# Layer 0 for four pairs at once in a conditional two-layer kernel, with the loads of x, the rings and two waits moved to fit

## The reference

```python
# layer 0: x is (128, 64, 512), w[subject] is 64x64, bias[subject] is 64
x = x + einsum('bct,bcd->bdt', x, weights[subjects]) + bias[subjects][:, :, None]
# layer 1: W is 512x512, A[k] is 16x512, Bm[k] is 512x16, scalings[k] a number
H = einsum('btd,od->bto', x, W)
delta = einsum('btr,bor->bto', einsum('btd,brd->btr', x, A[k]), Bm[k]) * scalings[k]
x = x + H + delta
```

## Time and profile before

| | value |
|---|---|
| median of three runs | 265.81 us |
| profiled execution | 265.84 us |
| its span | 264.2 us |
| TensorE busy | 241.5 us, 91% |
| VectorE, ScalarE, GpSimd busy | 145.2, 113.4, 82.2 us |
| mean granted TensorE clock | 0.978 |
| DMA | 36.69 MB, 139 GB/s in the mean |
| chain of waits, by engine | PE 86%, DVE 5%, DMA 3% |

### The profile page before, as it was taken

How to read it: one execution, slowest core, us unless ns; L and a number is a source line. 1 busy time by engine, 2 the same in 40 slices (tenths; PEclk the granted TensorE clock), 3 DMA queues, 4 the chain that set the end, 5 groups by cost and what they waited for, 6 DMA issues and landing times.

```text
span 264.2 us, 9940 instructions
## 1 busy us (share of the span) xinstructions
PE 241.5 (91%) x2929; PEld 194.7 (74%) x2930; DVE 145.2 (55%) x244; ACT 113.4 (43%) x189; POOL 82.2 (31%) x284
## 2 busy tenths in 40 slices
PE   0463999899999999999999999999999999999993
PEld 0442888688788888888888887888878887887882
DVE  5657557755565666755575655566675554433200
ACT  2154345544454445444464444544544443333411
POOL 6332342533324333332343332432333333320000
PEclk9977699999999999999999999999999999999999
DMA  6663144555545554655455545555564445552231
GB/s 114 152 186 105 43 133 134 160 139 148 154 144 156 157 159 139 180 154 144 121 177 155 141 140 146 157 152 159 139 188 149 144 127 179 155 156 79 70 78 42
DMA packets 25826, 36.69 MB, mean 139 GB/s; under 512 B 6736, under 2 KB 8784, under 8 KB 25808
## 3 DMA queue, kind: packets, MB, share of 16 engines
q1 hardware_dynamic: 20400, 28.06, 37.2%
q10 hardware_dynamic: 5408, 8.40, 12.3%
HBM read 19.67 MB, written 16.78 MB: 138 GB/s over the span
## 4 chain that ended last, share of the span: by engine, by line
PE 86%; DVE 5%; DMA 3%; issue 2%; ACT 1%; SPq 1%; ACTq 0%; DVEq 0%
PE ps L717 69%; PE ps L702 13%; PE ps L682 2%; DMA x_ring<-in_x_dram 2%; PE ps L664 2%; DVE m_lo L487 1%; DMA ids_i<-in_itok_B_dram 1%; DVE m_f L481 1%; ACT m_hi L563 1%; DVE x L494 0%; ACT x_hi L569 0%; DVE place L453 0%; DVE prec_n L388 0%; PE ps L654 0%; DVE x_lo L502 0%
## 5 line engine op out<-in xcount | busy, mean ns | idle before, releaser
L717 PE MATMUL ps<-m_hi,x_hi 128*128 x264 | 106.9, 405 | 0.8 <-DVE m_lo L487 0.8
L717 PE MATMUL ps<-m_lo,x_hi 128*128 x264 | 103.5, 392 | 0.0
L717 PE MATMUL ps<-m_hi,x_lo 128*128 x264 | 103.4, 392 | 0.0
L502 DVE TENSOR_TENSOR x_lo<-x,x_hi 128x512 fp32r<-128x512 f32 x64 | 44.5, 695 | 86.5 <-ACT x_hi L569 86.5
L359 POOL COPY p_pair<-p_all 64x64 f32 x128 | 45.6, 356 | 135.0 <-DVE x L494 62.0
L578 ACT ACTIVATE o_ring<-ps 128x512 f32<-128x512 f32 x60 | 35.8, 597 | 63.2 <-PE ps L717 62.9
L717 PEld LDWEIGHTS ps<-m_hi,x_hi 128*128 128x128 f32 x264 | 49.9, 189 | 12.6 <-issue 1.6
L717 PEld LDWEIGHTS ps<-m_hi,x_lo 128*128 128x128 f32 x264 | 49.8, 189 | 10.8
L569 ACT ACTIVATE x_hi<-x 128x512 fp32r<-128x512 f32 x64 | 40.4, 632 | 39.8 <-ACT o_ring L578 18.6
L717 PEld LDWEIGHTS ps<-m_lo,x_hi 128*128 128x128 f32 x264 | 49.9, 189 | 9.5
L702 PEld LDWEIGHTS ps<-p_pair,x_ring 64*64 64x64 f32 x2048 | 34.2, 139 | 18.2 <-issue 16.5
(11 more groups left out here) (81 smaller groups left out, 55.5 us busy)
## 6 DMA issues: line engine op xcount, KB each, us to landing
x_ring<-in_x_dram SPq DMA_DIRECT2D x128, 128.0 KB, 2.6
out_dram<-o_ring ACTq DMA_DIRECT2D x64, 128.0 KB, 2.4
out_dram<-o_ring SPq DMA_DIRECT2D x64, 128.0 KB, 2.5
o_ring<-in_L_cond_W_dram SPq DMA_DIRECT2D x4, 256.0 KB, 4.6
a_f<-in_L_cond_A_dram SPq DMA_DIRECT2D x8, 128.0 KB
b_nat<-in_L_cond_Bm_dram SPq DMA_DIRECT2D x1, 256.0 KB, 4.1
p_all<-in_L_cond_weights_dram SPq DMA_DIRECT2D x2, 128.0 KB, 4.3
bias_all<-in_fside_8xS_dram SPq DMA_DIRECT2D x1, 256.0 KB, 5.7
```

The costliest lines, as they stand in the source:

```text
L502: nc.vector.tensor_tensor(x1_lo[:, u % HELD], x1[:, u % 2], x1_hi[:, u % HELD], ALU.subtract).then_inc(x1_lo_ready, 1)
L717: mm = nc.tensor.matmul(ps[:, bank, :], part[:, u % HELD, c, :], m[:, ds(k * (TC * T) + c * T, T)], start=(c == 0 and part is x1_hi and m ...
```

## The change

It takes layer 0 for four pairs in one burst, at u = 2 and u = 6 only, for pairs j+2 to j+5 in the order j+2, j+4, j+3, j+5. The four results lie in the same four PSUM banks as before, two to a bank pair, in columns 0 to 255 and 256 to 511 (`l0_out`). `x1_add` waits for both results of its bank pair (`l0_count`).

SP loads x for the four pairs j+6 to j+9 in one step, at u = 2 and u = 6 (`load_quad`); `x_ring` still has four slots. `p_pair` and `bias_pair` have eight slots, and POOL waits for a slot accordingly. The batch numbers stand in a table of their own, `batch`, written by one DVE copy instead of two copies and a memset.

In the head, PE does both first layer-0 pairs after all four tiles of M and then `turn_b(1)`; layer 0 of pairs 2 and 3 moves from before layer 1 of pair 0 to before layer 1 of pair 1, and pairs 4 to 7 follow at pair 2. DVE and ACT make tiles 1 to 3 of M before the first `x1_add` and `x1_round`. PE's wait for M moves from u = 5 to u = 6, behind the burst. `load_a`, `a_round`, `a_split`, `turn_b` and the tiles of M keep their step.

```diff
@@ -45,9 +45,10 @@
     MIXED = K // 2
     XR = 4
     OR = 4
-    AHEAD = 6
+    PR = 8
+    L0_QUAD = 4
     HELD = 4
-    W_BATCH, W_AHEAD, W_SUBJECT, W_PLACE = 0, 2, 4, 6
+    W_SUBJECT, W_PLACE = 0, 2
 
     HEAD = 4
     BODY = 8
@@ -77,8 +78,8 @@
         w_nat = o_ring
         p_all = sb("p_all", [P, S, C])
         bias_all = sb("bias_all", [P, S, C])
-        p_pair = sb("p_pair", [P, XR, C])
-        bias_pair = sb("bias_pair", [P, XR, P])
+        p_pair = sb("p_pair", [P, PR, C])
+        bias_pair = sb("bias_pair", [P, PR, P])
         x1 = sb("x1", [P, 2, TC, P])
         x1_hi = sb("x1_hi", [P, HELD, TC, P], F32R)
         x1_lo = sb("x1_lo", [P, HELD, TC, P], F32R)
...
@@ -122,9 +124,16 @@
         ps = ctx.enter_context(nc.psum_tensor("ps", [P, 8, 512], F32))
         b_turned_at = ps[:, 4, :].rearrange("p (c n) -> p n c", c=TC)
 
-        def l0_banks(u):
-
-            return 6 * (u % 2)
+        def l0_count(j, u):
+
+            if isinstance(j, int) and j < L0_QUAD:
+                return j + 1
+            return j - u % L0_QUAD + (2, 4)[u % 2]
+
+        def l0_out(u):
+
+            cols = TC * C * (u // 2 % 2)
+            return ps[:, 6 * (u % 2):6 * (u % 2) + 2, cols:cols + TC * C]
 
 
         ids_in = sem("ids_in")
...
@@ -248,10 +251,17 @@
 
             def load_x(j, slot, b):
 
-                at_least(sp, l0_done, j - XR + 1)
+                at_least(sp, l0_done, j - XR + 1 if isinstance(j, int) and j < XR + L0_QUAD
+                         else j - XR - slot + (1, 3, 2, 4)[slot])
                 for half in range(2):
                     sp.dma_start(x_ring[C * half:C * half + C, slot, :], x[ds(b[half], 1)]
                                  .rearrange("b c t -> (b c) t")).then_inc(x_in[slot], 16)
+
+            def load_quad(j):
+
+                b = words(sp, regs, batch[0:1, ds(j * 2, 2 * L0_QUAD)], B - 1)
+                for i in (range(L0_QUAD) if isinstance(j, int) and j <= L0_QUAD else (0, 2, 1, 3)):
+                    load_x(j + i, i, b[2 * i:2 * i + 2])
 
 
             sp.wait_ge(order_ready, 1)
@@ -261,23 +271,20 @@
                          .to_broadcast([P, S * C]).rearrange("p (s d) -> p s d", s=S)).then_inc(bias_in, 16)
             load_w(3)
             sp.wait_ge(batches_ready, 1)
-            for j in range(XR):
-                load_x(j, j, words(sp, regs[:2], table[0:1, j * 8:j * 8 + 2], B - 1))
+            load_quad(0)
             load_a(1)
-            for j in range(XR, AHEAD):
-                load_x(j, j % XR, words(sp, regs[:2], table[0:1, j * 8:j * 8 + 2], B - 1))
+            load_quad(XR)
 
             def step(j, u, n):
                 if n is not None and u == HEAD - 1:
 
                     load_a(n + 2)
-                more = not isinstance(j, int) or j + AHEAD < PAIRS
-                b = words(sp, regs[:4 if more else 1], table[0:1, ds(j * 8, 4 if more else 1)], B - 1)
-                if more:
-                    load_x(j + AHEAD, (u + AHEAD) % XR, b[W_AHEAD:W_AHEAD + 2])
+                if u % L0_QUAD == 2 and (not isinstance(j, int) or j + XR + 2 < PAIRS):
+                    load_quad(j + XR + 2)
+                b, = words(sp, regs[:1], batch[0:1, ds(j * 2, 1)], B - 1)
 
                 sp.wait_ge(out_ready, j + 1)
-                sp.dma_start(out[ds(b[0], 1)].rearrange("b c t -> (b c) t"),
+                sp.dma_start(out[ds(b, 1)].rearrange("b c t -> (b c) t"),
                              o_ring[0:C, u % OR, :]).then_inc(even_out[u % OR], 16)
 
             pairs(sp, step, HEAD - 1)
@@ -350,10 +357,10 @@
                 if place_at is not None:
                     dup_b(place_at)
                     pool.wait_ge(b_dupped, place_at + 1)
-                slot = u % XR
-
-                at_least(pool, x1_ready, j - XR + 1)
-                s = words(pool, regs, table[0:1, ds(j * 8 + W_SUBJECT, 2)], S - 1)
+                slot = u % PR
+
+                at_least(pool, x1_ready, j - (PR - 1 if n is None else min(PR - 1, HEAD - 1 + (u - HEAD) % BODY)))
+                s = words(pool, regs, table[0:1, ds(j * 4 + W_SUBJECT, 2)], S - 1)
                 def place_p(half):
                     rows = slice(C * half, C * half + C)
                     nc.gpsimd.tensor_copy(p_pair[rows, slot, :], p_all[rows, ds(s[half], 1), :]
...
@@ -488,12 +491,11 @@
 
             def x1_add(j, u):
 
-                dve.wait_ge(l0_done, j + 1)
+                dve.wait_ge(l0_done, l0_count(j, u))
                 at_least(dve, x1_lo_ready, j - 1)
-                bank = l0_banks(u)
                 nc.vector.tensor_tensor(x1[:, u % 2].rearrange("p c (h d) -> p c h d", h=2),
-                                        ps[:, bank:bank + 2, 0:TC * C].rearrange("p h (c d) -> p c h d", c=TC),
-                                        bias_pair[:, u % XR, :].rearrange("p (h d) -> p h d", h=2).unsqueeze(1)
+                                        l0_out(u).rearrange("p h (c d) -> p c h d", c=TC),
+                                        bias_pair[:, u % PR, :].rearrange("p (h d) -> p h d", h=2).unsqueeze(1)
                                         .to_broadcast([P, TC, 2, C]), ALU.add).then_inc(x1_ready, 1)
 
             def x1_split(j, u):
@@ -509,25 +511,28 @@
             m_add(0, 0)
             m_add(1, 1)
             m_split(0, 0)
+            m_split(1, 1)
+            m_add(2, 2)
+            m_add(3, 3)
             x1_add(0, 0)
-            m_add(2, 2)
+            m_split(2, 2)
             x1_split(0, 0)
-            m_split(1, 1)
-            m_add(3, 3)
-            m_split(2, 2)
+            x1_add(1, 1)
             m_split(3, 3)
-            x1_add(1, 1)
             x1_split(1, 1)
 
             def step(j, u, n):
+                if n is None and j == 0:
+                    a_split(1)
+                    b_split(1)
                 if not isinstance(j, int) or j + 2 < PAIRS:
                     x1_add(j + 2, u + 2)
                     x1_split(j + 2, u + 2)
                 for place_at, chunk in split_at(j, u, n):
                     m_split(place_at * TC + chunk, chunk)
-                if makes_parts(j, u, n) is not None:
-                    a_split(makes_parts(j, u, n))
-                    b_split(makes_parts(j, u, n))
+                if n is not None and u == HEAD:
+                    a_split(n + 2)
+                    b_split(n + 2)
                 for place_at, chunk in tiles_of(j, u, n):
                     m_add(place_at * TC + chunk, chunk)
                 if n is None and j == HEAD - 1:
...
@@ -688,21 +696,29 @@
                 pe.wait_ge(x_in[slot], after(j, u, 32))
                 pe.wait_ge(pair_ready, j * 4 + 4)
 
-                at_least(pe, x1_ready, j - 1)
+                at_least(pe, x1_ready, j - 1 if isinstance(j, int) and j < L0_QUAD else j - u % L0_QUAD)
 
             def layer0(j, u):
 
                 slot = u % XR
-                bank = l0_banks(u)
+                x1_t = l0_out(u)
                 for c in range(TC):
                     for side in range(2):
                         for half in range(2):
                             rows = slice(C * half, C * half + C)
                             at = c * P + side * C
-                            mm = nc.tensor.matmul(ps[side * C:side * C + C, bank + half, c * C:c * C + C],
-                                                  x_ring[rows, slot, at:at + C], p_pair[rows, slot, :],
+                            mm = nc.tensor.matmul(x1_t[side * C:side * C + C, half, c * C:c * C + C],
+                                                  x_ring[rows, slot, at:at + C], p_pair[rows, u % PR, :],
                                                   start=True, stop=True)
                 mm.then_inc(l0_done, 1)
+
+            def l0_at(j, u):
+
+                if isinstance(j, int) and j == 1:
+                    return (1, 2)
+                if u % L0_QUAD == 2 and (not isinstance(j, int) or j + 2 < PAIRS):
+                    return (2, 4, 3, 5)
+                return ()
 
             def layer1(j, u, k, bank, done=l1_done, tiles_awaited=False):
 
@@ -727,28 +743,28 @@
             m_product(0, 0)
             m_product(1, 1)
             turn_w(2)
-            layer0_inputs(0, 0)
-            layer0(0, 0)
             turn_w(3)
             m_product(2, 2)
             m_product(3, 3)
             pe.wait_ge(others_ready, 2)
+            layer0_inputs(0, 0)
+            layer0(0, 0)
             layer0_inputs(1, 1)
             layer0(1, 1)
+            turn_b(1)
             regs = [pe.alloc_register(f"pe_word{i}") for i in range(2)]
 
             def step(j, u, n):
                 mixed = n_of_mixed(j) is not None
-                if u % 2 == 0 and (not isinstance(j, int) or j + 2 < PAIRS):
-                    layer0_inputs(j + 2, u + 2)
-                    layer0_inputs(j + 3, u + 3)
-                k = words(pe, regs[:2 if mixed else 1], table[0:1, ds(j * 8 + W_PLACE, 2 if mixed else 1)], K - 1)
```

(38 more changed lines are left out.)

## The result

The changed kernel takes **293.41 us** (median of 4 runs, 291.35 to 295.1) against 266.19 for the kernel before: a ratio of 1.102, 95% interval 1.092 to 1.113. It is slower, as forecast (290, range 272 to 299). Its profiled execution took 292.57 us.

The account below looks back on a forecast made before the run. TensorE, 91% busy, was taken to bound the kernel, with no slack on A's load path. Head -5.0, first body +2.7, five bodies +27.0, end -0.7 sum to +24 on 265.84, giving 290 us, range 272 to 299.

Parts of the forecast that it names:

- SP's queue: SP at u = 2: eight x loads take 5.4 us before the store, delaying A's load from B2 + 6.55 to 10.2.
- From A to B6: Load of A to burst at u = 6: 4.2 + 2.07 + 1.33 us plus 0.95 for extra waits; stall 4.4 us a body.
- The clock: PE's granted clock halves after the stall in each body, costing 1.4 us a body, bounds 0 and 2.5.
- The rival that the clock holds: Stalls in the loop, broken by the tile, do not lower PE's clock: 282 us instead of 290; chance 0.25.
- The other two rivals: SP's queue does not decide, 258 us, chance 0.13; or edges are bought dearly, 263 to 270 us, chance 0.10.
- The body: A loop body of eight pairs takes 33.9 us instead of 28.51, 5.4 more; five bodies 27.0.
- The first body: From the first burst of four to the next at u = 2: 32.6 us instead of 29.83, 2.7 more.
- The head: Before the loop, the first burst of four starts at 30.4 instead of 35.46: 5.0 us gained, between 3 and 6.5.
- The end: Behind the loop, three bursts' edges fewer: 0.7 us gained.
- The bursts' edges: Entering and leaving layer 0 bursts on PE costs 0.21 us together; fewer bursts gain 1.9 us, 0.7 behind the loop.
- The third rival's sum: A's load costs 1.5 us a body, clock stays: -7.7 + 9 to 12, given as 263 to 270 us; chance 0.10.

Follow-up runs that it names:

- e1: Changed kernel, but SP loads A at u = 2, ahead of the eight loads of x, instead of in the step behind them: 269.1 us, ratio 1.013.
- e2: Kernel before, but A's load issued behind the two loads of x of its step instead of ahead of them: 276.3 us, ratio 1.040.
- e8: Kernel before, but A's load issued behind the store of the step at u = 3: 283.8 us, ratio 1.076.
- e5: Changed kernel, A's load unmoved, but PE waits once for POOL's last pair and once for x1_ready before a burst of four: 292.0 us, ratio 1.101.
- e4: e1, but PE waits once for POOL's last pair and once for x1_ready before a burst of four: 260.7 us, ratio 0.983.
- e3: Changed kernel with 18 extra matmuls a body filling PE's stall at u = 5, around the first tile of M: 287.7 us, ratio 1.086.
- e6: e4, with M's first tile behind the burst of u = 6 and pair 7's x1_add ahead of the splits: 259.0 us, ratio 0.979.
- e7: Kernel before, but SP loads A in the step at u = 2, ahead of the loads of x: 264.9 us, ratio 1.000.

## Why the prediction was right, step by step

- **SP's queue.** Forecast: A at B2 + 10.2, between 9.7 and 10.8, with 5.4 us for the eight loads. Measured 10.67 in the body shown and 10.0 in the mean, with 5.5 us in four bodies of five. e1, e2 and e8 show that this is the cause: with A first the loss is nearly gone, and with A late in the kernel before, most of it appears without the change. The Trainium skill (DMA: Bandwidth & Descriptors, Issuing engines are not separate DMA queues) calls the time to initiate a DMA usually small relative to the DMA itself. One load of x took SP 0.69 us (5.49 / 8) of the 2.6 us to its landing; eight in a row took 5.5 us ahead of A's, and A did not come near B2 + 6.6.
- **From A to B6.** Forecast 4.2 + 2.07 + 1.33 + 0.95, so B6 at B2 + 18.75. Measured 18.6; in the body shown 4.32, 2.06 and 2.27 us. The 0.6 us in it for the waits of two more pairs is 0.7 by e5 (1.56 us instead of 2.27) and 0.8 by e4.
- **The clock.** Forecast 1.4 us a body; measured 1.5, isolated by e3. The rival that the clock holds, with a chance of 0.25, was wrong for the changed kernel, and right for most bodies of e2 and e8, whose stalls are shorter. The other two rivals fell with A's place and with B2 to B6.
- **The body.** Forecast 33.9 us; measured 34.0 (B2 from 64.30 to 234.33, five bodies).
- **The first body: the number by luck.** Forecast 32.6 us from the first burst of four to B2, with B6 held back by A and the clock falling there; measured 32.53 (31.77 to 64.30). But A held nothing back in this body, and B6 ran at full clock. The clock fell at the burst of 31.77 instead (3.60 us), behind the wait of 2.35 us, and B6 came 18.56 us after it, behind a stall of 1.27 us at the waits of four pairs. Rows 4 had been misread here: ACT's six waits for A are not once a body, but one in the setup and one in each of the last five bodies.
- **The head.** Forecast a gain of 5.0 us at the first burst of four; measured 35.39 - 31.77 = 3.6. x of pair 7 was forecast for 30.4 and landed at 31.0; POOL's biases, which the sum for the head leaves out, ended at 31.2, and the last waits brought the start to 31.77. POOL was not the cause by itself: in e4 and e5 the waits view puts the same wait (2.40 and 2.39 us) down to x, and the burst starts at 31.73 and 31.49.
- **The end.** Forecast 0.7 us less behind the loop; measured none (56.3 us from the last B2, as before). The wait for the last adapter's M at pair 53 kept its place while the burst in front of it, at pair 52, left, and costs 1.20 us. This wait was not in the prediction at all.
- **The bursts' edges.** They were to give 1.9 us, and with them PE's work alone was to take 14.35 + 13.75 = 28.1 us a body (the first term, by its own summands, is 14.39). e6 takes 27.66, against 28.37 in e7, where A is no hindrance either: 0.7 us less where 0.2 to 0.3 were forecast. A part of it is that a burst of four takes 2.02 us, and not 2 x 1.09; the rest was not taken apart. In the changed kernel, four pairs' waits made each burst of u = 2 0.3 us late, which I had named as a bound and taken at nothing, and the stall at B6 hid the rest.
- **The third rival's sum.** Its terms, -7.7 + 9 to 12, give 267 to 270 us, not 263 to 270.

The misses, 1.4 us in the head, 0.7 at the end and 0.1 in each of five bodies, add up to 2.6 of the 2.7 us between the forecast and the profiled execution.

## What to carry to other kernels

A transfer that is small and rare can be the one that counts: look up how long each waits in the issuing engine's queue, and before anything is batched in that queue, ask what stands behind the batch. Where two paths end together, taking one away gains nothing (e7) and lengthening it costs in full (e2), so the slack of the second path has to be read before an edit, not after. Many waits in a row have a price on the sequencer, 0.9 us a body at B6 and 0.3 at B2 by e1 and e4: where a counter tells of all items, wait for it once and not once an item.

## What the runs showed of the hardware that I had not expected

- A burst of 128 small matmuls takes 2.02 us at full clock by the chain of waits when PE comes to it without a stall (e6), less than two of 64 (1.09 each in the kernel before).
- PE's clock fell although a tile of M stood in the middle of the stall: 3.23 us idle, one matmul, 1.70 us idle, and then 0.56 in the next stretch. It fell in all five bodies, also where the first idle time was only 2.2 to 2.5 us. With the stall filled it stayed at 1.00.
- With shorter stalls the fall was irregular. Taking B2 to B6 over the 14.40 us of e7 as the stall, it was 1.6 to 2.5 us in e2, and the clock fell in one body of five (at 2.0); it was 2.3 to 3.4 us in e8, and the clock fell in two of five (at 3.4 and 3.2, but not in another body at 3.4). Each fall cost about 1.5 us.
- Eight loads issued in a row kept SP busy for 5.5 us in four bodies and for 6.4 us in the first of the five; there the third load started 1.8 us after the second (66.97 to 68.79) instead of 0.9, and why was not tried.
